# An attention block whose VectorE sums of two key blocks move two steps later, and whose joining transfer is issued behind the next pair's first sum

## What is computed

```python
q = (x @ wq_w + wq_b).reshape(bs, sl, Q_H, HEAD_DIM)
k = (x @ wk_w + wk_b).reshape(bs, sl, KV_H, HEAD_DIM)
v = (x @ wv_w + wv_b).reshape(bs, sl, KV_H, HEAD_DIM)
qg = q.reshape(bs, sl, KV_H, FACTOR, HEAD_DIM)
attn = jnp.einsum('bqhfd,bkhd->bhfqk', qg, k) * scale
att = jax.nn.softmax(attn, axis=-1)
a = jnp.einsum('bhfqk,bkhd->bqhfd', att, v)
return a.reshape(bs, sl, DIM) @ wo_w + wo_b
```

## Time and profile before

| | |
|---|---|
| median of three runs | 2808.56 us |
| profiled execution, its own time | 2811.7 us |
| span of its trace | 2809.9 us |
| PE busy | 2757.9 us (98%) |
| DVE busy | 2181.6 us (78%) |
| POOL busy | 1908.4 us (68%) |
| ACT busy | 1529.6 us (54%) |
| attention stage | about 640 to 2313 us of the span |

### The profile page before, as it was taken

The page is one execution under the profiler, slowest core; times in us unless marked ns, Lnnn a source line. Parts: engine busy times, 40 slices in busy tenths (PEclk is TensorE's granted clock), DMA queues, the critical chain, the costliest instruction groups (busy, mean ns, idle before and its releaser), DMA issues.

```text
span 2809.9 us, 48988 instructions
## 1 busy us (share of the span) xinstructions
PE 2757.9 (98%) x14654; PEld 1701.5 (61%) x14654; DVE 2181.6 (78%) x2801; ACT 1529.6 (54%) x2963; POOL 1908.4 (68%) x710
## 2 busy tenths in 40 slices
PE   7999999999999999999999999999999999999998
PEld 4788888884444444444444444444444447888886
DVE  4433434348999999999999999999999968667665
ACT  3111111116776767777777776776767754545543
POOL 2433333317999999999999999999999985111110
PEclk9999999999999999999999999999999999999998
DMA  7544443434434344344444433444444443333231
GB/s 263 182 143 136 144 140 132 136 115 136 91 87 100 85 87 99 87 90 94 94 91 89 96 88 87 96 90 90 90 98 90 91 130 102 107 113 105 98 112 68
DMA packets 167501, 307.05 MB, mean 109 GB/s; under 512 B 49985, under 2 KB 91393, under 8 KB 159361
## 3 DMA queue, kind: packets, MB, share of 16 engines
q1 hardware_dynamic: 158352, 240.05, 29.3%
q0 software_dynamic: 9072, 66.06, 11.5%
HBM read 159.12 MB, written 79.82 MB: 85 GB/s over the span
## 4 chain that ended last, share of the span: by engine, by line
PE 74%; DVE 2%; ACT 1%; issue 1%; POOL 0%; DVEq 0%; ACTq 0%; POOLq 0%
PE back_ps L1348 21%; PE back_ps L1362 18%; PE s_ps L1322 16%; PE s_ps L1838 12%; PE back_ps L1887 2%; PE back_ps L1379 2%; PE back_ps L1859 1%; PE back_ps L1906 1%; DVE mx L1237 1%; PE back_ps L1337 0%; ACT h_t L1695 0%; PE s_ps L1411 0%; DVE a_lo L1281 0%; DVE xn L1753 0%; DVE two_sum L1252 0%
## 5 line engine op out<-in xcount | busy, mean ns | idle before, releaser
L1218 ACT ACTIVATE p_t<-back_ps 128x512 f32<-128x512 f32 x2048 | 1113.9, 596 | 432.0 <-PE back_ps L1348 390.2
L1237 DVE TENSOR_REDUCE mx<-s_ps 128x1 f32<-128x1024 f32 x1002 | 1172.3, 1208 | 84.4 <-PE s_ps L1322 76.8
L1128 POOL TENSOR_TENSOR p_sum<-p_sum,p_t 128x2048 f32<-128x2048 f32 x254 | 1166.3, 4592 | 23.0 <-ACT p_t L1218 6.5
L1348 PE MATMUL back_ps<-q_st,k_st 98*128 98x512 f32 x2048 | 812.5, 437 | 3.4 <-POOL ones L1097 2.4
L1348 PEld LDWEIGHTS back_ps<-q_st,k_st 98*128 98x128 f32 x2048 | 344.2, 188 | 593.8 <-ACT p_t L1218 496.4
L1322 PE MATMUL s_ps<-k_st,q_st 96*128 96x512 f32 x2004 | 629.3, 395 | 0.6 <-DVE mx L1237 0.4
L1362 PE MATMUL back_ps<-p_t,v_sb 128*32 128x512 f32 x4096 | 546.4, 605 | 0.0
L1322 PEld LDWEIGHTS s_ps<-k_st,q_st 96*128 96x128 f32 x2004 | 379.1, 189 | 70.6 <-DVE mx L1237 3.4
L574 POOL TENSOR_TENSOR o_lo<-side,o_hi 128x512 fp32r<-128x512 f32 x80 | 104.2, 1302 | 321.7 <-ACT o_hi L544 321.6
L1128 POOL TENSOR_TENSOR p_sum<-p_t 128x2048 f32<-128x2048 f32 x64 | 313.4, 4897 | 9.6 <-ACT p_t L1218 9.6
L1252 DVE TENSOR_REDUCE two_sum<-p_t 128x512 f32<-128x1024 f32 x256 | 317.8, 1243 | 0.9 <-ACT p_t L1218 0.9
(11 more groups left out here) (152 smaller groups left out, 2920.8 us busy)
## 6 DMA issues: line engine op xcount, KB each, us to landing
p_sum<-two_sum POOLq DMA_DIRECT2D x63, 1024.0 KB, 6.9
q_st<-q_hi_d SPq DMA_DIRECT2D x128, 256.0 KB, 4.3
stage<-w_mod SPq DMA_DIRECT2D x48, 512.0 KB, 6.2
q_hi_d<-o_hi SPq DMA_DIRECT2D x64, 256.0 KB, 2.0
q_lo_d<-o_lo SPq DMA_DIRECT2D x64, 256.0 KB, 2.0
q_st<-q_lo_d SPq DMA_DIRECT2D x64, 256.0 KB, 4.1
att_d<-a_sb SPq DMA_DIRECT2D x128, 128.0 KB, 2.3
a_f<-att_d SPq DMA_DIRECT2D x32, 512.0 KB, 4.7
```

Of the source, the lines that this page charges most:

```text
L1128: nc.gpsimd.tensor_tensor(total, before, p_t[:, kt, :, :], ALU.add).then_inc(sum_done, 1)
L1218: nc.scalar.activation(p_t[:, s, c, :], st_ps[:, c % 2, :], ACT.Exp, scale=SCALE)\
L1237: nc.vector.tensor_reduce(mx[:, slot % 2, e:e + 1], s_ps[:, e % 2, :], AX_X, ALU.max)\
L1348: nc.tensor.matmul(st_ps[:, c % 2, :], k_st[:, slot // 2, s * P:(s + 1) * P], q_st[:, slot, jj, h * QW:(h + 1) * QW], start=True, stop=True)\
```

## The change

DVE's quarters 0 to 3 of a pair are summed at step 7 and at steps 0, 1 and 2 of the next pair, instead of steps 5, 6, 7 and 0. In the last pair they come at steps 6 and 7 and, for the last two, behind the loop. POOL issues `join` behind the first addition of the next pair instead of ahead of it. The waits themselves are unchanged.

```diff
-    TWO_STEPS = (5, 6, 7)
+    TWO_STEPS = {7: 0}
+    TWO_STEPS_NEXT = {0: 1, 1: 2, 2: 3}
+    TWO_STEPS_LAST = {6: 0, 7: 1}
...
         def do(pair, slot, it):
-            if not below(pair, 1):
-                join(pair - 1, (slot - 1) % 2)
             total = p_sum[:, slot % 2, :, :]
...
                 nc.gpsimd.tensor_tensor(total, before, p_t[:, kt, :, :], ALU.add).then_inc(sum_done, 1)
+                if n == 0 and not below(pair, 1):
+
+
+                    join(pair - 1, (slot - 1) % 2)
...
-                if s == 0 and not below(pair, 1):
-                    add_two(pair - 1, REP - 1)
-                if s in TWO_STEPS:
-                    add_two(pair, TWO_STEPS.index(s))
+                if s in TWO_STEPS_NEXT and not below(pair, 1):
+                    add_two(pair - 1, TWO_STEPS_NEXT[s])
+                here = TWO_STEPS_LAST if is_int(pair, NPAIR - 1) else TWO_STEPS
+                if s in here:
+                    add_two(pair, here[s])
...
         pairs(dve, do)
-        add_two(NPAIR - 1, REP - 1)
+        for c in range(len(TWO_STEPS_LAST), REP):
+            add_two(NPAIR - 1, c)
```

## The result

The changed kernel took 2877.85 us (median of 4 runs, 2875.54 to 2879.12) against 2808.39 us (4 runs, 2802.67 to 2810.24) before. The ratio is 1.025, 95% interval 1.0232 to 1.0268: 2.5% slower, 69 us. Forecast were 2884 us and 2862 to 2902.

What follows compares the result with a forecast made beforehand. PE was taken to bound the kernel, with DVE just in time. 73 us (61 pairs at 1.2) plus 2 us at the end made 75 us on 2808.6, so 2884 us, range 2862 to 2902.

Steps and rivals of the forecast that it cites:

- PE is the pacer and DVE's maxima are its only close limit: Attention: PE sets the pace at 3.10 us a step; DVE is ready just in time, so making it later costs.
- E + 1.27 us: Attention: a PE step cannot start earlier than 1.27 us after DVE's second maximum, two steps before, ends at E.
- 1.2 us a pair, 73 us: Pairs 2 to 62: DVE steps with a sum and a division piece delay PE 1.2 us in each of 61 pairs.
- ACT costs nothing: ACT's block 3 exponential waits for the fourth quarter, about 1.1 us later, covered by PE's 0.69 us lateness and slack.
- POOL costs nothing and gains nothing: POOL's idle 0.67 us before the join goes, but nothing waits for POOL, so gain and cost are 0.
- Pairs 0 and 1 balance: Pairs without division: three stretched steps before, three after; balance 0, with 0.5 us either way.
- The end, 2 us: Last pair: later join delays the four sums and the `up_w` load behind them; 2 us, bounds 0 and 4.9.
- POOL is the pacer: Rival: POOL's 0.67 us wait vanishes in 61 pairs, 41 us less, 2770 us; chance 0.04.
- the lateness is absorbed: Rival: PE's steps have hidden slack or DVE runs mixed steps faster; only the end remains, 2811 us; chance 0.06.

Runs made afterwards that it cites:

- mixed step: Kernel before with the division's pieces one step earlier (0, 1, 2), so step 0 holds the fourth quarter's sum and `den_t`: 2833.6 us, ratio 1.0100.
- unmixed steps: Changed kernel with sums at steps 6, 7, 0 and 1 and the division at 2, 3 and 4: 2814.5 us, ratio 1.0030.
- four other orders: Before, only join moved: 2837.8 us; changed, sums 6, 7, 0, 1, division 2-4: 2814.5; changed, only division 2-4: 2873.0; before, division 0-2: 2833.6.
- quarter waits: Changed kernel with each quarter's exponential on ACT waiting for its own quarter's sum, not all four: 2878.1 us, ratio 1.0257.
- its line moved: POOL's wait for and scaling of `up_w` put behind pair 62's `divide`; kernel before: 2806.3 us, ratio 0.9998; same edit in changed kernel: 2871.8 us, 1.0235.
- first two runs: Changed kernel with the join put back ahead of the first addition: 2876.1 us; kernel before with only the join moved behind it: 2837.8 us.

## Why the prediction was right, step by step

- **PE is the pacer and DVE's maxima are its only close limit: right.** The new wait is on L1328, twice a pair, in steps 2 and 3 (160 and 114 entries in the list). The mixed step in the kernel before and the unmixed steps in the changed one switch the loss on and off with the join untouched.
- **E + 1.27 us: right.** It fits both long steps to 0.03 us, and gave 0.45, 0.08, 1.02 and 0.52 us a pair for four other orders, measured 0.43, 0.08, 1.02 and 0.47. Of these the first hit the amount but named the wrong steps.
- **1.2 us a pair, 73 us: slightly too much.** Measured 1.12 in 60 pairs, 67 us; pair 62, which the forecast counted as the 61st, got 0.7 us shorter. PE's step 2 got 0.69 us longer, as forecast (3.80 against 3.11 in the pair shown; 0.65 in the mean). Step 2 holds 1271.57 - 1268.06 = 3.51 us of DVE work and not 3.65: `rden_c` took 0.15 in a row without waits, where I had taken its duration of 0.22, and the maxima behind it 2.21 instead of 2.26.
- **ACT costs nothing: right**, shown by the quarter waits. The forecast had the exponential of block 3 start with PE's step 3 (1039.21 and 1039.25); it started 0.09 us behind it. The wait for the fourth quarter made it 0.46 us later than the finer waits did, and the period was 27.14 us with them, as long as without.
- **POOL costs nothing and gains nothing: right in this order only.** Its 0.67 us of idle time are gone and it waits 113.0 / 58 = 1.9 us a pair for exponentials (1.8 forecast). But the place of the join is not free by itself: with the old sums it costs 0.43 us a pair. I had only asked what waits for the join in the new order.
- **Pairs 0 and 1 balance: right.** From the second L1362 row of the attention to step 7 of pair 1 it took 41.61 us before and 41.57 after.
- **The end, 2 us: 2.8 in the trace, a value taken inside bounds and with a row misread.** The forecast read the first sum at 2294.81 as waiting for the join. Its row names ACT, and in the mixed step and in the kernel before with its line moved the sums start at the same 10.9 us ahead of the last denominator matmul, in the second with the join 1.5 us earlier. Before, the join was not what they waited for; in the changed kernel it is, and the wait is longer than the 7.55 us that the forecast used: issued at 2356.14, first sum at 2364.49, 8.35 us. The sums of the last pair so end 5.0 us later against that matmul, not 4.4. Of this 3.8 reached the issue of the load, because SP came to it only at 2300.87 before, and 2.9 its landing (2379.82, 5.1 us ahead of the first addition of the last stage on DVE at 2384.95, as before with 2312.33 and 2317.44). The chain is shown by the moved line; the size rests on one execution each.
- The rivals *POOL is the pacer* and *the lateness is absorbed* are refuted by the first two runs and by the mixed step: an engine busy for 97% of the stretch gave back its idle time and nothing got faster.

## What to carry to other kernels

When one engine sets the pace and another is nearly full beside it, the work of the second is not free anywhere: add it up from the last point at which it waits to each result that the pacer needs, and compare with the pacer's own time to there. A step is no unit for this. Work moved out of a crowded step into the next one bought a seventh of what it cost (0.10 of 0.69 us), while work moved to where the engine idled bought nearly all of it (all but 0.08 of 1.12 us a pair). Two halves of a change can each be a loss alone without the losses adding up (0.43 and 1.13 us a pair, 1.12 together); time them apart before one is judged.

## What the runs showed of the hardware

DVE's subtraction with two operands in SBUF (128x1024, `a_lo`, once each in pairs 62 and 63) took 5.50 us in pair 62 before, 3.60 in the changed kernel and 2.00 in the kernel with only the sums moved. In each it ended 1.1 us after a POOL operation did, whenever it had begun. The kernel before and then the one with the sums moved, POOL and DVE:

```profile
2265.84 4.55 POOL L1128 TENSOR_TENSOR p_sum<-p_sum,p_t 128x2048 f32<-128x2048 f32 x1
2270.35 2.30 POOL L1139 TENSOR_TENSOR a_sb<-rden,num_sb 128x512 f32<-128x512 f32 x1
```

```profile
2265.97 5.50 DVE L1281 TENSOR_TENSOR a_lo<-a_f,a_hi 128x1024 fp32r<-128x1024 f32 x1
```

```profile
2328.34 4.87 POOL L1130 TENSOR_TENSOR p_sum<-p_t 128x2048 f32<-128x2048 f32 x1
2333.36 5.42 POOL L1130 TENSOR_TENSOR p_sum<-p_sum,p_t 128x2048 f32<-128x2048 f32 x1
```

```profile
2332.31 2.00 DVE L1283 TENSOR_TENSOR a_lo<-a_f,a_hi 128x1024 fp32r<-128x1024 f32 x1
```

POOL's addition ended at 2270.39 and 2333.21, DVE's subtraction at 2271.47 and 2334.31, and POOL's next operation took 2.30 instead of 1.31 us and 5.42 instead of 4.57. In the changed kernel the subtraction did not come next: it began 1.3 us before an addition ended (at 2333.77), and POOL's multiplication still went ahead of it. It ended 1.09 us after that multiplication (2333.46 + 1.55 = 2335.01):

```profile
2333.46 1.55 POOL L1143 TENSOR_TENSOR a_sb<-rden,num_sb 128x512 f32<-128x512 f32 x1
```

```profile
2332.50 3.60 DVE L1285 TENSOR_TENSOR a_lo<-a_f,a_hi 128x1024 fp32r<-128x1024 f32 x1
```

One operand in SBUF is no protection by itself. The normalisation of the last stage (`xn`, 128x1024, one such operand and two numbers per partition) ended 0.54 or 0.55 us after the POOL operation beside which it had begun, the first time in each of the ten kernels, and took 1.43 to 4.05 us. The quarter sums and the maxima, reductions with one operand, kept 1.24 and 1.21 us beside the same additions. The Trainium skill (GPSIMD Engine Reference, Specifications) says that GpSimd's SBUF interfaces are shared with VectorE, and contended when a VectorE instruction has two SBUF inputs or runs in a 2-port perf mode. The trace agrees for the two inputs, and its durations fit two engines that take turns by whole operations. The mode in which the normalisation ran is not shown by any run here. PE waited 2.02 us for the subtraction before and 0.28 us after, and pair 62 is the one pair that got shorter (28.58 to 27.84 us); that the second follows from the first was not tried by itself.
